# An adaLN block with gated linear recurrence and experts on one Trainium2 core: gate products and decay series reordered in the attention stage

## The reference

```python
mod = (_silu(L0_c) @ L0_wmod).reshape(B, 6, 1, -1)           # sa, ca, ga, sb, cb, gb
h = _layernorm(x) * (1 + ca) + sa
xn = rmsnorm(h, norm1_w)
left = gelu(xn @ left_W + left_b)
u = causal_depthwise_conv(xn @ right_W + right_b, conv_w, conv_b)   # 4 taps
r = sigmoid(u @ ga_W + ga_b);  i = sigmoid(u @ gx_W + gx_b)
log_a = -8 * softplus(a_param) * r
a = exp(log_a);  b = sqrt(-expm1(2 * log_a)) * (i * u)
right = scan of h = a * h_before + b over the 256 tokens of a batch
x1 = left * right @ out_W + out_b + h
attn = (gelu(rmsnorm(x1) @ up1_W + up1_b) * (rmsnorm(x1) @ up2_W + up2_b)) @ down_W + down_b + x1
x = x + ga * attn
h = _layernorm(x) * (1 + cb) + sb
x = x + gb * (top-2 mixture of 8 experts(h) + h)
```

## Time and profile before

| | us |
|---|---|
| median of 3 runs (lowest to highest) | 275.64 (274.57 to 280.36) |
| the profiled execution | 276.33 |
| its span, first to last instruction | 274.6 |
| PE busy | 263.4 (96%) |
| DVE busy | 194.7 (71%) |
| ACT busy | 173.8 (63%) |
| POOL busy | 125.2 (46%) |

### The profile page before, as it was taken

The page is one execution under the profiler, slowest core; times in us unless marked ns, Lnnn a source line. Parts: engine busy times, 40 slices in busy tenths (PEclk is TensorE's granted clock), DMA queues, the critical chain, the costliest instruction groups (busy, mean ns, idle before and its releaser), DMA issues.

```text
span 274.6 us, 4511 instructions
## 1 busy us (share of the span) xinstructions
PE 263.4 (96%) x1593; PEld 219.4 (80%) x1594; DVE 194.7 (71%) x459; ACT 173.8 (63%) x295; POOL 125.2 (46%) x104
## 2 busy tenths in 40 slices
PE   8999999999999999999999899999999999999991
PEld 3756554357688788877588799999999999999991
DVE  3858699739838678879945879785858677785630
ACT  4347795686289336980878767939578493948310
POOL 7103603000142212368275534876483838568464
PEclk9989997999999999999999999999999999999998
DMA  5990000000004757216176668869093866717044
GB/s 186 379 353 14 0 1 0 0 2 0 0 2 172 243 165 168 54 68 212 62 250 220 168 188 239 233 201 311 35 336 104 276 189 178 225 19 218 14 54 51
DMA packets 32838, 38.40 MB, mean 140 GB/s; under 512 B 7964, under 2 KB 28444, under 8 KB 32796
## 3 DMA queue, kind: packets, MB, share of 16 engines
q1 hardware_dynamic: 27184, 30.56, 35.2%
q0 software_dynamic: 4928, 7.44, 11.9%
q10 hardware_dynamic: 700, 0.07, 0.2%
HBM read 32.10 MB, written 8.90 MB: 149 GB/s over the span
## 4 chain that ended last, share of the span: by engine, by line
PE 65%; DVE 14%; ACT 12%; issue 4%; POOL 2%; DMA 1%; POOLq 1%; another core or an unknown queue 0%; DVEq 0%; ACTq 0%
PE bank L1019 19%; PE bank L1062 14%; PE bank L700 6%; PE bank L616 4%; PE bank L799 4%; PE bank L1056 2%; PE bank L647 2%; PE bank L1055 2%; PE bank L627 2%; PE bank L902 2%; DVE u L1588 2%; PE bank L1006 2%; ACT tmp L1246 1%; DMA out_x<-y_tok,meta 1%; POOL out_x L2123 1%
## 5 line engine op out<-in xcount | busy, mean ns | idle before, releaser
L2123 POOL DMA_INDIRECT out_x<-y_tok,meta x24 | 50.9, 2121 | 36.0 <-DVE y_tok L1949 20.9
L1062 PE MATMUL bank<-w_hi,own 128*128 128x256 f32 x256 | 48.8, 284 | 0.2 <-DVE own L1932 0.2
L1390 ACT ACTIVATE own_raw<-bank,b1c 128x320 f32<-128x320 f32 x64 | 33.4, 533 | 15.7 <-PE bank L1019 12.0
L1931 DVE TENSOR_TENSOR own<-own_raw,own 128x256 fp32r<-128x256 f32 x64 | 27.1, 424 | 22.1 <-issue 11.8
L1062 PEld LDWEIGHTS bank<-w_hi,own 128*128 128x128 f32 x256 | 41.1, 191 | 0.7 <-DVE own L1932 0.6
L1019 PE MATMUL bank<-xe_hi,w_hi 128*128 128x320 f32 x128 | 40.0, 313 | 1.5 <-DVE xe_lo L1927 1.0
L1019 PE MATMUL bank<-xe_lo,w_hi 128*128 128x320 f32 x128 | 39.6, 309 | 0.0
L1019 PE MATMUL bank<-xe_hi,w_lo 128*128 128x320 f32 x128 | 39.5, 309 | 0.0
L1062 PE MATMUL bank<-w_lo,own 128*128 128x256 f32 x128 | 36.2, 283 | 0.0
L2113 POOL DMA_INDIRECT gb_rows<-gb_table,meta x24 | 24.8, 1033 | 11.5 <-issue 6.7
L1396 ACT ACTIVATE own<-own_raw 128x320 fp32r<-128x320 f32 x64 | 29.6, 480 | 0.0
(11 more groups left out here) (252 smaller groups left out, 607.1 us busy)
## 6 DMA issues: line engine op xcount, KB each, us to landing
e_raw<-in_L_ffn_w SPq DMA_DIRECT2D x16, 1024.0 KB
x_rows<-in_L_attn_x SPq DMA_DIRECT2D x1, 2560.0 KB
xe_tok<-x_rows SPq DMA_DIRECT2D x7, 256.0 KB
raw_m<-in_L_attn_up_W SPq DMA_DIRECT2D x2, 768.0 KB, 9.5
x_tok<-in_L_attn_x SPq DMA_DIRECT2D x2, 512.0 KB, 5.2
out_x<-x_tok SPq DMA_DIRECT2D x1, 1024.0 KB, 5.2
xe_tok<-x_rows SPq DMA_DIRECT2D x7, 128.0 KB
wmod<-in_L_wmod SPq DMA_DIRECT2D x1, 768.0 KB, 11.6
```

Of the source, the lines that this page charges most:

```text
L1062: ins = nc.tensor.matmul(bank[b][0:n, 0:D], l, r, start=False, stop=(c == KE - 1 and t == 2))
L1390: nc.scalar.activation(own_raw[:, f % 4, :], bank[b][:, 0:CAP], ACT.Gelu, bias=b1c[:, g:g + 1]).then_inc(drained[b], 1)
L1931: nc.vector.tensor_tensor(own_lo[e % 2][:, f, :], own_raw[:, f % 4, 0:whole], own_hi[e % 2][:, f, 0:whole].bitcast(F32), ALU.subtract)
L2123: nc.gpsimd.indirect_dma_start(out_rows, bass.IndirectOffsetOnAxis(ap=ids[0:n, e, k, E:E + 1], axis=0), y_tok[e % 2][0:n, k, :], None, com ...
```

## The change

1. PE makes both decay-gate products of a half ahead of its input-gate products. In half 0 the right products of half 1 move between them: decay 0, decay 1, right(1,0), input 0, input 1, right(1,1).
2. The series is cut in two. `softplus_begins` (7 instructions) stands in DVE's stream ahead of the convolutions of half 0; `softplus_ends` (11 instructions) stands ahead of `rms_apply` of half 1, where it was behind it. ACT's small Sigmoid moves to the prologue, ahead of `m_hi(0)`.
3. The input gate is taken as 0.5 * (1 + tanh(z / 2)): Tanh on ACT, `(t + 1) * u` on DVE, and the factor goes into the Sqrt (scale 0.25). One small DVE instruction is added for half the bias.
4. Half 1's m=1 right product is read by DVE (`right_of(1)`) and no longer by ACT; DVE's `inputs(0)` moves behind `conv(2)`.
5. The squares of x1 of half 0 are made by DVE (tensor_tensor, behind each `x1_of`) and no longer by ACT; `inputs(1)` is cut in two around them, and ACT's `roots(1)` moves ahead of `mean_root(("ms2", 0), 0)`.
6. POOL's splitting of b2 waits for `n_lo_done` and no longer for the convolutions.

The core of the diff:

```diff
-    take_gates(0)
-    take_side("right", 1)
+    take_gates(0, 0)
+    order.take(("right", 1, 0), drains=2)
+    take_gates(0, 1)
+    order.take(("right", 1, 1), drains=2)
...
-            gates(0)
-            side("right", 0, 1)
+            gates(0, 0)
+            side("right", 0, 1, [0])
+            gates(0, 1)
+            side("right", 0, 1, [1])
...
+            act.wait_ge(abs_done, 1)
+            nc.scalar.activation(lru[:, 1, :], lru[:, 1, :], ACT.Sigmoid).then_inc(abs_done, 1)
             m_hi(0)
...
-            def gate_functions(hf, m):
...
+            def decay_gate(hf, m):
+                b, ps = full(("gate", hf, m, 0))
+                nc.scalar.activation(tmp[:, hf * KH + m, :], ps[:], ACT.Sigmoid, bias=C("ga_b", m)).then_inc(drained[b], 1)
+
+            def input_gate(hf, m):
+
+                b, ps = full(("gate", hf, m, 1))
+                nc.scalar.activation(tmp[:, 4 + hf * KH + m, :], ps[:], ACT.Tanh, bias=lru[:, 0, m:m + 1], scale=0.5).then_inc(drained[b], 1)
...
-            gate_functions(0, 0)
-            gate_functions(0, 1)
+            decay_gate(0, 0)
+            decay_gate(0, 1)
             act.wait_ge(softplus_done, 1)
             decays(0, [0])
-            right(1, 1)
+            input_gate(0, 0)
+            input_gate(0, 1)
             decays(0, [1])
             roots(0)
-            for m in range(KH):
-                gate_functions(1, m)
+            decay_gate(1, 0)
+            decay_gate(1, 1)
             decays(1, [0])
-            squares(0, "out", 1, [0])
+            input_gate(1, 0)
+            input_gate(1, 1)
             decays(1, [1])
-            squares(0, "out", 1, [1])
+            roots(1)
             mean_root(("ms2", 0), 0)
-            roots(1)
...
+            def softplus_ends():
+                for k in range(SERIES - 1 - FIRST, 0, -1):
+                    term(k)
                 st.link(nc.vector.scalar_tensor_tensor(out=lru[:, 4, :], in0=lru[:, 4, :], scalar=1.0, in1=lru[:, 2, :], op0=ALU.add, op1=ALU.mult))
                 st.link(nc.vector.tensor_scalar(lru[:, 3, :], a_par, 0.0, 0.5, ALU.max, ALU.mult))
                 st.link(nc.vector.tensor_tensor(lru[:, 3, :], lru[:, 3, :], lru[:, 4, :], ALU.add))
...
             rms_inverse(("ms", 1), 1, 2)
+            softplus_ends()
             rms_apply(("rb", 1), 1, ("xh", 2), "norm1_w")
-            softplus()
...
-            ready = inputs(0)
             right_of(0)
             conv(2)
+            ready = inputs(0)
+            right_of(1)
             conv(3)
...
-            st.need(inputs(1))
-            x1_of(0)
+            inputs(1, [0])
+            for dt in range(KD):
+                x1_of(0, [dt])
+                until_drained(("out", 0, dt))
+                nc.vector.tensor_tensor(square[:, dt, hs[0]], hT[:, dt, hs[0]], hT[:, dt, hs[0]], ALU.mult).then_inc(square_done, 1)
             rms_inverse(("ms2", 0), 0, 3)
+            ready = inputs(1, [1])
...
-            pool.wait_ge(conv_done, NH * KH)
+            pool.wait_ge(n_lo_done, KD)
```

More of the change, by code:

```diff
@@ L108, in adaln_block, with take_gates @@
     order.take(("ms", 1))
-    def take_gates(hf):
+    def take_gates(hf, g):
         for m in range(KH):
[L112 to L115, removed]
+            order.take(("gate", hf, m, g))
+            if hf == 0 and m == 0 and g == 0:
+                order.take(("rb", 1), drains=2)
     def take_out(hf):
@@ L119, in take_out @@
             order.take(("out", hf, dt))
-    take_gates(0)
-    take_side("right", 1)
+    take_gates(0, 0)
+    order.take(("right", 1, 0), drains=2)
+    take_gates(0, 1)
+    order.take(("right", 1, 1), drains=2)
     order.take("mod_b")
     order.take(("left", 1, 0))
-    take_gates(1)
+    take_gates(1, 0)
+    take_gates(1, 1)
     take_out(0)
@@ L732, in _, with gates @@
             mean_square(("ms", 1), 1, 1)
-            def gates(hf):
+            def gates(hf, g):
                 pe.wait_ge(conv_done, KH * (hf + 1))
-                for g in range(2):
-                    pe.wait_ge(a_in[2 + g], 16)
+                pe.wait_ge(a_in[2 + g], 16)
                 for m in range(KH):
[L739 to L743, removed]
+                    whole_product(("gate", hf, m, g), 2 + g, m, u, hf)
+                    if hf == 0 and m == 0 and g == 0:
+                        pe.wait_ge(rinv_done, 2)
+                        spread(("rb", 1), 1)
             def out_products(hf):
@@ L763, in _ @@
             end(modulation(ps, second[KD:]), mod_bank)
-            gates(1)
+            gates(1, 0)
+            gates(1, 1)
             pe.wait_ge(a_in[4], 16)
@@ L1184, in left @@
                     nc.scalar.activation(gel[:, m, hs[hf]], ps[:], ACT.Gelu, bias=C("left_b", m)).then_inc(drained[b], 1)
-            def gate_functions(hf, m):
-                for g, bias in enumerate(("ga_b", "gx_b")):
-                    b, ps = full(("gate", hf, m, g))
-                    nc.scalar.activation(tmp[:, 4 * g + hf * KH + m, :], ps[:], ACT.Sigmoid, bias=C(bias, m)).then_inc(drained[b], 1)
+            def decay_gate(hf, m):
[4 more added lines that the diff above has]
+                nc.scalar.activation(tmp[:, 4 + hf * KH + m, :], ps[:], ACT.Tanh, bias=lru[:, 0, m:m + 1], scale=0.5).then_inc(drained[b], 1)
             def decays(hf, ms=range(KH)):
@@ L1202, in roots @@
                     act.wait_ge(lru_out, 2 * k + 2)
-                    nc.scalar.activation(tmp[:, k, :], tmp[:, k, :], ACT.Sqrt).then_inc(root_out, 1)
+                    nc.scalar.activation(tmp[:, k, :], tmp[:, k, :], ACT.Sqrt, scale=0.25).then_inc(root_out, 1)
             def keep_x(hf):
@@ L1507, in _, with term, softplus_begins @@
             a_par = a_col[:]
-            def softplus():
+            SERIES, FIRST = 9, 2
+            def term(k):
+                st.link(nc.vector.scalar_tensor_tensor(out=lru[:, 4, :], in0=lru[:, 4, :], scalar=1.0 / (2 * k + 1), in1=lru[:, 3, :],
+                                                       op0=ALU.add, op1=ALU.mult))
+            def softplus_begins():
                 dve.wait_ge(abs_done, 2)
@@ L1514, in softplus @@
                 st.link(nc.vector.tensor_tensor(lru[:, 3, :], lru[:, 2, :], lru[:, 2, :], ALU.mult))
-                SERIES = 9
                 st.link(nc.vector.tensor_scalar(lru[:, 4, :], lru[:, 3, :], 1.0 / (2 * SERIES + 1), None, ALU.mult))
-                for k in range(SERIES - 1, 0, -1):
-                    st.link(nc.vector.scalar_tensor_tensor(out=lru[:, 4, :], in0=lru[:, 4, :], scalar=1.0 / (2 * k + 1), in1=lru[:, 3, :],
-                                                           op0=ALU.add, op1=ALU.mult))
+                for k in range(SERIES - 1, SERIES - 1 - FIRST, -1):
+                    term(k)
+            def softplus_ends():
+                for k in range(SERIES - 1 - FIRST, 0, -1):
+                    term(k)
                 st.link(nc.vector.scalar_tensor_tensor(out=lru[:, 4, :], in0=lru[:, 4, :], scalar=1.0, in1=lru[:, 2, :], op0=ALU.add, op1=ALU.mult))
@@ L1577, in _ @@
             nc.vector.tensor_tensor(lru[:, 7, :], lru[:, 0, :], cols[:, row["conv_b"]:row["conv_b"] + KH], ALU.add).then_inc(lru_done, 1)
+            dve.wait_ge(lru_done, 1)
+            nc.vector.tensor_scalar(lru[:, 0, :], cols[:, row["gx_b"]:row["gx_b"] + KH], 0.5, None, ALU.mult).then_inc(lru_done, 1)
             dve.wait_ge(par_in, 16)
@@ L1582, in _ @@
             ln_apply(x_tiles(1), xhat, 2).then_inc(xhat_done, 1)
+            softplus_begins()
             def conv(n):
@@ L1629, in u_of, with inputs @@
                 return ui[:, k % KH, hs[k // KH]]
[L1631 to L1634, removed]
+            def inputs(hf, ms=range(KH)):
+                for m in ms:
+                    k = hf * KH + m
+                    until_drained(("gate", hf, m, 1))
+                    last = st.mark(nc.vector.scalar_tensor_tensor(out=u_of(k), in0=tmp[:, 4 + k, :], scalar=1.0, in1=u[:, m, hs[hf]],
+                                                                  op0=ALU.add, op1=ALU.mult))
                 return last
@@ L1647, in recur, with x1_of @@
                 nc.vector.tensor_tensor(y_all[:, k % KH, hs[k // KH]], gel[:, k % KH, hs[k // KH]], u_of(k), ALU.mult).then_inc(y_done, 1)
-            def x1_of(hf):
-                for dt in range(KD):
+            def x1_of(hf, dts=range(KD)):
+                for dt in dts:
                     b, ps = full(("out", hf, dt))
@@ L1678, in _ @@
             nc.vector.tensor_copy(b1c[:], ps[:, 0:E * KE]).then_inc(drained[b], 1)
+            st.need(ready)
             recur(2)
```

4 lines of the change are left out of this document (1 added, 3 removed).

## The result

The changed kernel takes 279.15 us (median of 6 runs, 277.93 to 281.26) against 275.84 (median of 6 runs) for the kernel before: a ratio of 1.0118, 95% interval 1.0082 to 1.0153. It is slower by about 3.3 us, which is within 2%. Run again beside other kernels, it came to 1.018 (1.0109 to 1.0251). The ratios compare fast executions with fast ones; the medians are of all. The forecast was 278.9.

What follows compares the result with a forecast made beforehand. PE was taken to bound the kernel, busy 263.4 of 274.6 us. Terms 3.65 + 1.7 - 0.36 - 1.0 - 0.74 = +3.25 on the profiled 276.33 gave 279.6; the median, 0.7 lower, 278.9; range 274.3 to 281.5.

Steps and rivals of the forecast that it cites:

- The rest of the series ahead of xn: Before xn of half 1: POOL's low-weight instructions hold two series instructions on DVE, PE idles at right(1,0), +3.65 us.
- The bound of 2.5: Same place: if scalar_tensor_tensor is not held beside POOL, PE's idle is 2.5 us instead of 3.65.
- Clock behind that idle: PE behind its idle before right(1,0): the clock falls to 1.2 GHz, +1.7 us, bounded by 0 and 3.4.
- The wait before the gates of half 1: PE ahead of the gates of half 1: its wait for DVE's last convolution goes, -0.36 us.
- The clock fall there: Gates of half 1 on PE: the fall to 1.2 GHz may go or stay, -1.0 us, from 0 to -1.95.
- Squares on DVE: PE before the mean square of x1: the wait for ACT's squares goes, -0.74 us.
- The rest: Tanh, merged multiply, Sqrt scale, y of half 0 and POOL's b2 work: no cost to PE, 0 us.
- Prologue: Ahead of the first convolution: seven series instructions, the moved Sigmoid and its table load are hidden, 0 us.
- Rival A: Series ahead of xn: nothing is held by POOL, xn is on time, -2.1 us, 273.5 us; chance 0.14.
- Rival C: PE's wait in front of the experts hides some of the late xn, within 0.5 us of before, 275.6; chance 0.08.
- Rival B: PE at 1.2 GHz from its restart through the modulation and again in half 1's gates: +5.95, 281.6 us; chance 0.10.

Runs made afterwards that it cites:

- experiment 1: Changed kernel with the eleven series instructions behind the xn of half 1 again, as before the change: ratio 1.0004 to the kernel before.
- experiment 2: Changed kernel with POOL's two low-weight instructions waiting for the end of the series, not for the convolutions of half 0: ratio 1.0038 to the kernel before.
- experiment 6: Changed kernel with only the second of POOL's low-weight instructions waiting for the end of the series: ratio 0.9925 to the kernel before.
- experiment 11: Changed kernel with POOL's two low-weight instructions replaced by zero fills that read nothing: 272.98 us, one execution.
- experiment 5: Changed kernel with the first of POOL's low-weight instructions done twice, so three stand beside the series: ratio 1.0258 to the kernel before.
- experiment 3: Kernel before with only the series moved and the small Sigmoid in the prologue, PE's order untouched: ratio 1.0005 to the kernel before.
- experiment 4: Changed kernel with PE's old order in half 0, all four gate products and then both right products: ratio 1.0101 to the kernel before.
- experiment 9: Changed kernel with POOL's splitting of b2 waiting for the convolutions again, as before the change: 284.75 us, one execution.
- experiment 10: Changed kernel with the squares of x1 of half 0 on ACT again and its two roots behind the mean root: 283.03 us, one execution.

## Why the prediction was right, step by step

- *The rest of the series ahead of xn, +3.65.* Right: 3.61 us, with both holds at the predicted instructions (experiments 1, 2, 6 and 11 take the hold away or shorten it, experiment 5 lengthens it, experiments 3 and 4 separate it from PE's order). The bound of 2.5 for the case that scalar_tensor_tensor passes is ruled out.
- *Clock behind that idle, +1.7 (0 to 3.4).* The range was right, the single value is a mean of unlike cases. Behind this wait of 3.6 us, two profiles show no fall (the changed kernel twice), and two do: experiment 9 lost about 1.6 us in right(1,0) (3.56 against 1.95) and experiment 10 about 2.95. Experiment 5 lost about 1.5 us behind its longer wait. I cannot say from the profile when it will fall. That my one value came out near the measured time was luck.
- *The wait before the gates of half 1, -0.36.* Right. *The clock fall there, -1.0 (0 to -1.95).* The changed kernel's profiles have none, but neither has experiment 3, which has the old order and the small matmuls. It is no effect of the change that I could show; I counted as a gain what comes and goes with the execution. The fall was also priced a little high: the same gates take 8.83 us with it and 7.13 without, 1.7 us.
- *Squares on DVE, -0.74.* The wait is gone, but not by this: experiment 10 has the squares on ACT and no wait, so the squares on DVE brought nothing there. The wait in the profile of the kernel before hangs on the fall of the clock in the gates, which brought ACT its last gates late: its last Sigmoid starts 23.16 us behind the first spread there and 21.65 us in experiment 3, which has all but the series as before, full clock in the gates, and no wait before the mean square. Experiment 3 waits 0.91 us before the output product, for y of half 0, which the changed kernel has not. So the two waits that the change removes come to 0.36 + 0.74 = 1.10 us in the one profile and 0.15 + 0.91 = 1.06 in the other. The total was right, the cause of the larger part was not, and which part of the change brings y earlier was not taken apart. Experiment 9 gives the place of the b2 work about 0.3 us of it.
- *The rest, 0.* Mis-sized for the b2 work: I had it hidden with 0.1 us to spare, and it cost PE about 0.4 us of wait for v_lo. What the same move gave back at recur(0) I had left out too.
- *Prologue, 0.* Right: the seven instructions left DVE 0.20 us of its wait, and the Sqrt table was back 0.15 us before the root.
- *Rival A* failed as a forecast. Its price of 2.1 us agrees with experiment 6, where the hold is nearly gone and the change brings 0.75%, but 1.0 of it was the clock term above, so the agreement is partly luck. *Rival C* fell with the result itself, 3.3 us slower. *Rival B* was not met in full; experiment 10's execution comes nearest.

The sum, +3.25, came out at +3.3. That is closer than its terms deserve: the waits that are shown come to 3.61 - 1.1 + 0.4 = 2.9. Waits are not quite time: neighbouring products overlap by some 0.17 us, and a wait takes that away too. By the two spreads the stage itself lost 1.9 us (31.71 against 29.81 in experiment 3), or up to 2.2 if the wait of experiment 3 before right(1,0), which the kernel before has not, is taken out. With the 0.4 that is 2.3 to 2.6 us. The interval of the ratio, 2.3 to 4.2 us, holds it. The clock, which moves single executions by some 2 us either way, can account for the rest, but no run shows that it does.

What stays open: between the start of the experts (141.62 us against 141.52 before, in the chain that ends last) and the end of the span the profiled execution lost another 1.5 us, half of it in the first experts' handoffs and half behind the issue of the last transfer. I made no experiment on that part, and the changed kernel's second profile ended at 275.6.

## What to carry to other kernels

Before small instructions are moved ahead of one that PE waits for, look at what POOL does at that time. Beside POOL's tensor_tensor, a DVE instruction with two SBUF inputs cost here what was left of POOL's instruction, whatever its own size, and two POOL instructions back to back held two of them. A DVE tensor_scalar that reads one SBUF tensor was held as well (0.87 us for 128 x 2; 1.30 and 1.37 for 128 x 256); those that read a PSUM bank were not (the four of the modulation take 1.90 us with POOL beside them and in experiment 2 without it). The profile draws this as a long instruction; no list of waits has it. A moved product also takes with it the slack that its old place had: read from the trace how late its input may be (here 3.5 us), and compare with what the same change puts ahead of that input.

## What the runs showed of the hardware that I had not expected

- Zero fills by POOL (2.69 us for two of 128 x 1536) did not hold DVE's two-input instructions at all (experiment 11).
- The time of one kernel mostly goes with TensorE's clock: of 49 executions of the kernel before, the 9 with a mean granted clock under 0.975 took 281.2 us in the mean and the 17 over 0.985 took 276.1. It is not all: one took 283.70 us at 0.990. Part of it is a stretch at 1.2 GHz in the prologue that some executions have and others not, with the same instructions there: from 10 to 20 us the clock was 1.00 in the changed kernel's profile, 0.83 in that of experiment 10 and 0.50 in those of experiments 1 and 9.
- The same pause of 3.6 us before the same product was followed by full clock in two executions and by a stretch at 1.2 GHz in two others (experiments 9 and 10, whose kernels differ from the changed one only further on).
